# The leftovers' low part in VectorE's step of a fused GroupNorm and convolution kernel, and the order of four products in W1's shift

## What is computed

```python
def _L0_conv_ref(x):                  # a Hadamard matrix over the channels
    y = pad(x_as_pixels_by_channels, 256) @ H     # H = hadamard(256) / 16
    return y[:, :192]                             # back to channels first

def _L1_conv_ref(x, W1, b1, g1, beta1, W2, b2, g2, beta2, W3, b3):
    h = einsum('bhwc,oc->bhwo', h, W1) + b1
    h = gelu(_layernorm(h, g1, beta1), approximate=False)
    h = einsum('bhwc,oc->bhwo', h, W2) + b2
    h = gelu(_layernorm(h, g2, beta2), approximate=False)
    return einsum('bhwc,oc->bhwo', h, W3) + b3

x = x + _L0_conv_ref(_gn(x))
x = x + _L1_conv_ref(_gn(x), W1, b1, ..., W3, b3)
```

## Time and profile before

| | |
|---|---|
| median of 3 runs | 913.5 us (913.45 to 914.02) |
| profiled execution, its own time | 913.21 us |
| its span (first to last instruction) | 911.4 us |
| PE busy | 850.6 us, 93% of the span |
| DVE busy | 814.8 us, 89% |
| ACT busy | 803.1 us, 88% |
| POOL busy | 567.5 us, 62% |
| share of PE in the chain that ended last | 80% |
| share of DVE in it | 7% |
| mean DMA rate | 88 GB/s |

### The profile page before, as it was taken

One profiled execution on the slowest core, in us unless ns is written; L12 is line 12 of the kernel. 1 busy time (PEld: TensorE's weight loads), 2 busy tenths in 40 slices (PEclk: granted clock), 3 DMA queues, 4 the chain that ended last, 5 costly groups with the idle time before them and its releaser, 6 DMA issues.

```text
span 911.4 us, 22670 instructions
## 1 busy us (share of the span) xinstructions
PE 850.6 (93%) x8601; PEld 565.6 (62%) x8601; DVE 814.8 (89%) x1382; ACT 803.1 (88%) x2348; POOL 567.5 (62%) x413
## 2 busy tenths in 40 slices
PE   0658999999999999999999999999999989899997
PEld 0226666666666666666666666666666656566663
DVE  5899999999999999999999999999999879875465
ACT  1946999999999999999999999999999979888982
POOL 0223676766766766776757666766667656757760
PEclk9877999999999999999999999999999999999999
DMA  9541042242332242332432232322422111121214
GB/s 256 146 118 59 2 126 87 87 126 73 105 92 86 87 126 70 108 106 73 119 94 90 86 108 71 116 96 78 135 73 71 37 35 36 36 72 35 71 36 105
DMA packets 55420, 80.46 MB, mean 88 GB/s; under 512 B 17936, under 2 KB 18064, under 8 KB 55184
## 3 DMA queue, kind: packets, MB, share of 16 engines
q1 hardware_dynamic: 55312, 79.01, 28.8%
HBM read 40.45 MB, written 38.54 MB: 87 GB/s over the span
## 4 chain that ended last, share of the span: by engine, by line
PE 80%; DVE 7%; ACT 5%; POOL 3%; SPq 2%; issue 1%; DMA 1%; DVEq 0%; ACTq 0%
PE tm L553 20%; PE tp L565 10%; PE tm L548 9%; PE hl L458 7%; PE tp L572 4%; PE hl L386 4%; PE tm L542 4%; PE hl L463 4%; PE hl L487 3%; PE hl L482 3%; PE hl L391 3%; PE hl L408 3%; POOL ge_lo L971 2%; PE hl L403 2%; PE hl L337 2%; ACT z L733 1%
## 5 line engine op out<-in xcount | busy, mean ns | idle before, releaser
L971 POOL TENSOR_TENSOR ge_lo<-ge,ge_hi 128x512 f16<-128x512 f32 (+1 forms) x190 | 327.6, 1735 | 83.0 <-ACT ge_hi L763 83.0
L963 POOL TENSOR_TENSOR rs<-ssq,neg_half 128x4 f32<-128x4 f32 x196 | 213.4, 1089 | 195.1 <-ACT z L733 194.7
L733 ACT ACTIVATE z<-tm 128x194 f32<-128x194 f32 x784 | 251.4, 336 | 43.6 <-PE tm L553 40.8
L1300 DVE TENSOR_TENSOR z<-tm,rs 128x768 f32<-128x768 f32 x196 | 185.7, 948 | 30.0 <-POOL rs L963 29.9
L745 ACT ACTIVATE ge<-tp,par 128x512 f32<-128x512 f32 x196 | 154.2, 787 | 22.2 <-PE tp L565 21.5
L733 ACT ACTIVATION_READ_ACCUMULATOR z<-tm 128x1 f32 x784 | 166.4, 212 | 0.0
L763 ACT ACTIVATE ge_hi<-ge 128x512 f16<-128x512 f32 (+1 forms) x190 | 160.3, 851 | 4.2
L565 PE MATMUL tp<-cst,z 128*128 128x128 f32 x784 | 124.2, 281 | 9.2 <-DVE z L1300 7.6
L565 PEld LDWEIGHTS tp<-cst,z 128*128 128x128 f32 x784 | 86.0, 143 | 35.0 <-DVE z L1300 25.3
L553 PE MATMUL tm<-w_hi,ge_hi 128*128 128x192 f16 x392 | 97.5, 249 | 0.0
L1169 DVE BATCH_NORM_STATS2 bn<-X 128x6 f32<-128x512 f32 x144 | 96.6, 682 | 0.5
(11 more groups left out here) (196 smaller groups left out, 2079.8 us busy)
## 6 DMA issues: line engine op xcount, KB each, us to landing
X<-x SPq DMA_DIRECT2D x48, 512.0 KB, 4.2
out<-X SPq DMA_DIRECT2D x48, 512.0 KB, 3.3
X<-x SPq DMA_DIRECT2D x96, 128.0 KB, 4.1
out<-X SPq DMA_DIRECT2D x96, 128.0 KB, 3.2
X<-weights SPq DMA_DIRECT2D x1, 1024.0 KB, 8.8
XL<-x SPq DMA_DIRECT2D x16, 32.0 KB, 3.3
XL<-x SPq DMA_DIRECT2D x32, 8.0 KB, 2.8
out<-left_ab SPq DMA_DIRECT2D x2, 256.0 KB, 3.6
```

Source lines behind the costliest of these rows:

```text
L733: last = nc.scalar.activation(z[n][:, 2 * h + k, i * TW:(i + 1) * TW], tm[h][:, i, k * TW:(k + 1) * TW], ACT.Square, scale=float(C) ** -0. ...
L963: nc.gpsimd.tensor_tensor(rs[n][:, 2 * h:2 * h + 2, :], ssq[n][:, 2 * h:2 * h + 2, :], neg_half[0:TT, 0:4].rearrange("p (i k) -> p i k", i=2),
L971: nc.gpsimd.tensor_tensor(ge_lo[n][:, g % 2, PART[h], :], ge[n][:, PART[h], :], ge_hi[n][:, g % 2, PART[h], :], ALU.subtract).then_inc(s_g ...
L1300: nc.vector.tensor_tensor(z[n][:, 2 * h:2 * h + 2, 0:2 * C].rearrange("p k (i o) -> p i k o", i=2), tm[h][:, :, 0:2 * TW].rearrange("p i ( ...
```

## The change

Two edits. In DVE's `step`, `scaled_left_lo(h_unit(g + 1))` moves from behind `scaled_lo(h_unit(g + 1), 2)` to ahead of `final_ab(g - 2)`. In PE's `w1_shift` the two loops are exchanged, so that products of half 0 and half 1 alternate; the operands of each product and its flags stay.

```diff
@@ w1_shift
-                for i, terms in enumerate(((0, 1), (3, 2))):
-                    for k, rows in enumerate(terms):
+                for k in range(2):
+                    for i, rows in enumerate(((0, 3), (1, 2))[k]):
                         last = nc.tensor.matmul(gp[64 * i:64 * i + 2 * B, 0:C], gshift2[:, k, :], w32[:, rows, :],
                                                 start=(k == 0), stop=(k == 1), skip_group_check=True)
@@ DVE's step
                 stats_x1(h_unit(g), 1)
+                scaled_left_lo(h_unit(g + 1))
                 final_ab(g - 2)
                 x1_split_lo(unit_at(g + 1), 0)
                 normalise(g - 1, 1, 0)
                 x1_split_lo(unit_at(g + 1), 2)
                 scaled_lo(h_unit(g + 1), 2)
-                scaled_left_lo(h_unit(g + 1))
                 normalise(g - 1, 1, 1)
```

## The result

| | us |
|---|---|
| before, median of 6 runs of this comparison | 912.38 |
| changed kernel, median | 904.47 |
| ratio after to before (95% interval) | 0.9919 (0.9892 to 0.9945) |
| profiled execution after, its own time | 904.73 |
| its span | 902.9 (before 911.4) |

One of the six runs of the changed kernel took 4270.68 us at a granted clock of 0.184, which no run here explains; it is not in the ratio, and the median of the other five is 904.20 us. The change saves 7.4 us of 912.4 by the ratio, 8.5 us by the two spans.

What follows compares the result with a forecast made beforehand. PE, busy 93% of the span, was taken as the bound, with gains only where it stands still. Idle time 5.20 plus slow stretch 3.21 gives 8.4, with the shift 8.5: 913.5 - 8.5 = 905.0 us, range 903 to 915.5.

Steps and rivals of the forecast that it cites:

- Where the time lay: DVE's two L1134 in steps 39 and 42: stretched by POOL's L971 to 3.22 us against 0.44, delaying z for PE.
- Idle time, 2 x 2.60 us: PE ahead of L565, twice: its wait for DVE's z goes entirely, saving 5.20 us.
- slow stretch, 1.57 + 1.64 us: PE from L565 to L403 in steps 40 and 43: the lower clock after standing still goes, saving 3.21 us.
- the small overlap at the start of L565: PE at L565: may come back too, giving the range's upper gain of 8.8 us; not in the sum.
- L1289 absorbs the 0.36 us in the late steps: DVE, step 39: the moved L1134's 0.36 us vanish in L1289's existing wait for POOL; it still ends at 734.95.
- The steady steps: Steps 3 to 36, 12 of them: L1289 leads L971 by 0.08 us, DVE runs 0.20 us later, PE loses 0.
- the first rival: Steps 3 to 36: POOL wins the port, L1289 waits, PE loses 0.86 us a step; 915.3 us or more, chance 0.19.
- W1's shift: PE's sixteen product groups: old order already overlaps two halves; alternating saves a few nanoseconds a group, 0.1 us in all.
- third rival: Steps 40 to 42: new POOL waits or ACT give back 2 to 4 us of the gain; 908 us, chance 0.13.

Runs made afterwards that it cites:

- The late move alone: Kernel before with scaled_left_lo (xsl_lo) moved ahead of final_ab in steps 39 and 42 only, products in the old order: 903.07 us, ratio 0.9902.
- the reduction in the old place: Kernel before, xsl_lo written in steps 39 and 42 by a one-element maximum, without scaling and subtraction, in L1134's place: 904.21 us, ratio 0.9916.
- the experiment with the busy PE: Kernel before with 11 extra 512-column matmuls on PE in steps 40 and 43, ahead of the waiting transposes: 909.30 us, ratio 0.9976.

## Why the prediction was right

- **Where the time lay** (L1134 in POOL's way in steps 39 and 42, and nowhere else): right. The late move alone and the reduction in the old place each give all of it (last two spacings 51.55 and 49.35, 51.55 and 49.34 us).
- **Idle time, 2 x 2.60 us, and slow stretch, 1.57 + 1.64 us, 8.4 in all:** right in kind, slightly small in size. The spacings give 8.84 us. L565 comes 2.75 and 2.76 us earlier, 5.5 us instead of 5.2: the small overlap at the start of L565, which I had kept in the range and left out of the sum, comes back as well. The other 3.3 us lie behind L565, and the experiment with the busy PE puts the clock at 3.2 us.
- **The time itself, 905.0 us against 904.47:** nearer than it deserves. I subtracted 8.5 us from a median of 913.5 us; the kernel before had 912.38 in the comparison, and a single execution scatters by several microseconds (907.36 to 914.02 for the kernel before). That the two numbers agree to 0.5 us is luck; that the traces give 8.8 us against a forecast of 8.5 is not.
- **L1289 absorbs the 0.36 us in the late steps:** right. In step 39 it took 1.65 us instead of 2.00, in step 42 1.58 instead of 1.94, and ended 1.08 us after L971 both times.
- **The steady steps, L1289's lead of 0.08 us, DVE keeps the port, everything 0.20 us later, PE untouched:** right. The lead was 0.081 to 0.086, L971 2.22 us instead of 2.02, the spacing 50.70 as before. The last normalise now waits 0.24 us for rs, as worked out.
- **The edge of the first rival:** wrong in place. I put it at a lead of about 0.06 us, from the moments at which each wants its data; it is at about 0.012 us, by the starts. So the margin was about 0.07 us, not 0.02, and the chance of 0.19 rested on too small a margin. Its price was right: L565 was to come 0.86 us later by the first loss and up to 1.6 us by the second, and came 0.88 and 1.56 us later (0.81 and 1.40 us of them idle).
- **W1's shift:** right, 6 to 7 ns for each group.
- **Given back later (third rival):** it did not come. Neither between steps 40 and 42 nor behind step 42 does PE lose any of it again.

## What to carry to other kernels

A DVE instruction whose duration is a multiple of that of its equals, with no idle time ahead of it, has waited inside for POOL: look at what POOL ran then, and move the shorter one out of the way before cutting work. When such an instruction is moved, compute in every kind of step what it pushes towards POOL's instructions, for the loser pays the other's whole length, and a few hundredths of a microsecond decide it. An engine with spare time is no cover for a delay where its next instruction must win a race.

## What the runs showed of the hardware that was not expected

- Where DVE's x_lo or xs_lo and POOL's ge_lo excluded each other, the start of the instruction decided, with the edge within about 0.01 us of a tie: leads of 0.012 to 0.018 us kept DVE's 1024-column instruction at 1.28 us, a lag of 0.04 us made it 2.20 us, and leads of 0.001 to 0.012 us made its 512-column instruction 2.69 us instead of 0.74.
- A tensor_scalar from float32 to float16 with one SBUF tensor as input waits for POOL (3.21 us for two), a reduction of the same 64 and 32 columns does not (0.30 us for two).
- Four float32 products of 32 weight columns for two column blocks of the array take the same time in either order: 0.85 us when both of the first block stand ahead of both of the second, 0.84 us alternated, where eight full-array instructions take 1.57 us. That products of the two blocks overlap in the old order too is inferred from this, as said above.
- A stand of 2.60 us in an otherwise busy PE was followed by a stretch at the lower clock that cost 1.6 us; with the stand filled by other matmuls the granted clock stayed at 1.00.
- A memset of two columns runs beside the DVE instruction that follows it and delays it by 0.01 us; a statistics instruction over 8 columns delays it by about 0.07 us, one over 64 columns by about 0.13 us.
